# Attention stage of an image-and-text block: sums of the probabilities taken from spare columns of the values, inverses on 48x41 through memory, mask pieces in fp32r

## The reference

```python
h = concatenate([image_tokens(x), fake_quant(table)[x_txt]], axis=1)      # (32, 164, 192)
h = h + attn(layernorm(h))
h = h + kan(kan(layernorm(h), w1), w2)

def attn(x):                                  # q, k, v = x @ W + b, split in 12 heads of 16
    scores = einsum('bhqd,bhkd->bhqk', q, k) * 0.25
    scores = where(abs(i - j) <= 64, scores, -inf)
    out = einsum('bhqk,bhkd->bhqd', softmax(scores), v)
    return out.reshape(B, N, 192) @ Wo + bo
```

## Time and profile before

| | |
|---|---|
| median of 3 runs | 2768.41 us |
| profiled execution | 2763.8 us, span 2762.1 us |
| TensorE matmul busy | 2544.0 us (92% of the span) |
| VectorE busy | 1870.7 us (68%) |
| ScalarE busy | 1354.8 us (49%) |
| GpSimd busy | 242.1 us (9%) |
| mean granted TensorE clock | 0.953 |

### The profile page before, as it was taken

The page is one execution under the profiler, slowest core; times in us unless marked ns, Lnnn a source line. Parts: engine busy times, 40 slices in busy tenths (PEclk is TensorE's granted clock), DMA queues, the critical chain, the costliest instruction groups (busy, mean ns, idle before and its releaser), DMA issues.

```text
span 2762.1 us, 52306 instructions
## 1 busy us (share of the span) xinstructions
PE 2544.0 (92%) x21673; PEld 2308.9 (84%) x21673; DVE 1870.7 (68%) x2148; ACT 1354.8 (49%) x1292; POOL 242.1 (9%) x147
## 2 busy tenths in 40 slices
PE   8959985898889889559999999999999999999999
PEld 6736684776667667459999999999999999999999
DVE  7849913655556566386766767666877777777774
ACT  2238801322223223255353443537977777777771
POOL 2202201000000000031121212100000000000000
PEclk9989996988989999879999999999999999999999
DMA  3435513000000000000000000003000000000000
GB/s 113 128 90 148 139 33 136 10 17 9 17 9 17 14 12 13 14 12 24 17 27 23 17 23 17 23 28 115 28 20 23 24 20 21 25 20 20 27 16 9
DMA packets 83907, 103.44 MB, mean 37 GB/s; under 512 B 8919, under 2 KB 75111, under 8 KB 83047
## 3 DMA queue, kind: packets, MB, share of 16 engines
q1 hardware_dynamic: 80167, 90.99, 10.9%
q0 software_dynamic: 3616, 10.54, 1.5%
HBM read 71.14 MB, written 30.36 MB: 37 GB/s over the span
## 4 chain that ended last, share of the span: by engine, by line
PE 56%; DVE 1%; issue 0%; DMA 0%; POOL 0%; ACT 0%; SPq 0%; POOLq 0%; DVEq 0%
PE spline_acc L1620 31%; PE spline_acc L1603 8%; PE spline_acc L1602 8%; PE spline_acc L1604 8%; PE spline_xT L1583 0%; DMA spline_x<-h_scr 0%; DVE spline_weights_low L1327 0%; DVE spline_xn L569 0%; DVE spline_f L1360 0%; DVE spline_t L1348 0%; DVE spline_b L1343 0%; DVE spline_b L1337 0%; DVE spline_a L1332 0%; POOL spline_rstd L1299 0%; ACT spline_a L1491 0%
## 5 line engine op out<-in xcount | busy, mean ns | idle before, releaser
L1620 PE MATMUL spline_acc<-spline_weights,spline_f 128*128 128x192 f32 x5248 | 853.0, 326 | 0.0
L1620 PEld LDWEIGHTS spline_acc<-spline_weights,spline_f 128*128 128x128 f32 x5248 | 852.8, 190 | 0.0
L1368 DVE SCALAR_TENSOR_TENSOR spline_f<-spline_n,spline_b 128x2048 f32<-128x2048 f32 x164 | 376.0, 2293 | 183.7 <-PE spline_acc L1620 181.9
L1602 PE MATMUL spline_acc<-spline_f,spline_weights_high 128*128 128x328 f32 x1536 | 479.8, 312 | 7.2 <-DVE spline_f L1360 7.2
L1603 PE MATMUL spline_acc<-spline_f,spline_weights_high 128*128 128x328 f32 x1536 | 482.4, 314 | 0.0
L1604 PE MATMUL spline_acc<-spline_f,spline_weights_low 128*128 128x328 f32 x1536 | 476.2, 310 | 0.0
L1602 PEld LDWEIGHTS spline_acc<-spline_f,spline_weights_high 128*128 128x128 f32 x1536 | 289.9, 189 | 7.4 <-issue 7.4
L1603 PEld LDWEIGHTS spline_acc<-spline_f,spline_weights_high 128*128 128x128 f32 x1536 | 289.1, 188 | 0.0
L1604 PEld LDWEIGHTS spline_acc<-spline_f,spline_weights_low 128*128 128x128 f32 x1536 | 288.7, 188 | 0.0
L1360 DVE SCALAR_TENSOR_TENSOR spline_f<-spline_n,spline_a 128x984 fp32r<-128x984 f32 x128 | 151.1, 1180 | 200.1 <-PE spline_acc L1604 198.4
L912 ACT ACTIVATE attend_probs<-scores_by_key 82x1968 f32<-82x1968 f32 x64 | 115.7, 1807 | 316.2 <-PE scores_by_key L1040 316.2
(11 more groups left out here) (154 smaller groups left out, 3567.3 us busy)
## 6 DMA issues: line engine op xcount, KB each, us to landing
sample_pos<-pos_scr SPq DMA_DIRECT2D x32, 540.0 KB, 4.4
hid_scr<-spline_hid SPq DMA_DIRECT2D x64, 164.0 KB, 1.8
spline_xn<-hid_scr SPq DMA_DIRECT2D x41, 256.0 KB, 3.1
pix_scr<-stem_by_pixel SPq DMA_DIRECT2D x32, 225.0 KB, 2.5
sample_h<-pix_scr POOLq DMA_DIRECT2D x32, 225.0 KB, 4.4
spline_weights_raw<-w SPq DMA_DIRECT2D x1, 6144.0 KB, 22.0
spline_weights<-w SPq DMA_DIRECT2D x4, 1536.0 KB, 6.1
h_scr<-attend_h SPq DMA_DIRECT2D x16, 246.0 KB
```

What stands on the lines that cost most here:

```text
L1368: nc.vector.scalar_tensor_tensor(f2[i][:], n_[u][:], MAGIC + i, b_[u][:], ALU.is_equal, ALU.mult).then_inc(f_ready, 1)
L1602: nc.tensor.matmul(z, high, x_high, start=start, stop=False)
L1620: last = nc.tensor.matmul(z, f2[i][:, r * P:(r + 1) * P], w2[:, i, r, :], start=(i == 0 and r == 0), stop=(i == 3 and r == 4 * CH - 1))
```

## The change

- **Masks.** `piece` and `mask` are copied to fp32r instead of bf16, and the windows get even widths: 222 x 3 and 250 x 3 columns of the four pieces instead of 218 x 3 and 246 x 3.
- **Sums.** The 16 columns of `attend_v` that were zero beside each head's 16 values are one. The product with the values so leaves the sums in rows 16 to 31 of every group of 32; `mix(..., True)`, the tile of ones and `SUM` are gone.
- **Inverses through memory.** ScalarE copies the whole product (`mix_out`, 128x492) to `mixed[i]`. SyncE stores 4 rows of it to memory, loads them as 48x41, VectorE inverts them (one reciprocal), SyncE stores 48x41 and loads it with four transfers, each repeated over 32 rows, into `spread[i]`; VectorE then multiplies `mixed[i]` by `spread[i]` (`weigh`). Each step waits for the one before.
- **Order.** A sample is inverted and weighed in the half after its own: VectorE's `invert` after the second `maximum`, `weigh` behind `low_max`, `residual` at the end of the half. `project_out` moves from behind q = 1 to behind the second wk projection (first half) or behind `values` (second half), ahead of `mix`. The uses of the banks are renumbered, 16 for a pair.
- **Bias.** The bias of the output is a row of `wo` (row 16 of the first group, where the weighed product is sum times inverse). GpSimd's addition and `bo` are gone; the residual is loaded from memory a second time.
- **Queues.** SyncE keeps the constants, the spline weights and the round trips of the sums. GpSimd now issues, for every pair, the store of the result, three loads of the residual and three loads of the input.
- `values` moves from VectorE to ScalarE; `double` writes columns 16 to 18 instead of 3 to 5.

The core of the diff, in this order: the numbering of the banks, `invert` of SyncE, `pair` of GpSimd, of VectorE and of TensorE (behind q = 3):

```diff
-    NX = 18
+    NX = 16
+    SUMS, PART = 48, HEADS * TOK // 48
-        X, Q, K_, V = (0, 1), (3, 4, 5), (8, 9, 10), (13, 16)
-        Y, SUM, MAX, MIX = (2, 12), (6, 14), (7, 15), (11, 17)
+        X, Q, K_, V = (0, 1), (2, 3, 4), (6, 7, 9), (11, 13)
+        Y, MAX, MIX = (8, 14), (5, 12), (10, 15)
...
+            def invert(t, i):
+                sp.wait_ge(mix_ready, 2 * t + i + 1)
+                sp.dma_start(total_scr[i], mixed[i][DH:P:32, :]).then_inc(total_out[i], 16)
+                sp.wait_ge(total_out[i], 16 * t + 16)
+                sp.dma_start(total[i][0:SUMS, :], total_scr[i].rearrange("j (k n) -> (j k) n", n=PART)
+                             ).then_inc(total_in[i], 16)
+                sp.wait_ge(inverted, 2 * t + i + 1)
+                sp.dma_start(rec_scr[i].rearrange("j (k n) -> (j k) n", n=PART), rec[i][0:SUMS, :]
+                             ).then_inc(rec_out[i], 16)
+                sp.wait_ge(rec_out[i], 16 * t + 16)
+                for j in range(4):
+                    sp.dma_start(spread[i][32 * j:32 * j + 32, :],
+                                 rec_scr[i, j:j + 1, :].rearrange("a n -> (a n)").partition_broadcast(32)
+                                 ).then_inc(spread_in[i], 16)
...
+            def pair(tt, u, more=True):
+                t = 2 * tt + u
                 pool.wait_ge(ln, LN_STEPS * t + LN_VAR)
                 pool.tensor_tensor(rstd[0:ROWS, :], ve[0:ROWS, :], minus_half[0:ROWS, :], ALU.pow).then_inc(pow_done, 1)
                 if not (isinstance(tt, int) and tt == 0):
-                    pool.wait_ge(h_ready, 2 * t - 2)
-                pool.tensor_tensor(resid[u][0:ROWS], x[u][0:ROWS],
-                                   bo[0:ROWS, :, :].to_broadcast([ROWS, 4, D]), ALU.add).then_inc(resid_ready, 1)
+                    leave(t - 2, u)
+                load(pool, resid[u], resid_in[u], t)
+                if more:
+                    pool.wait_ge(xn_ready, t + 1)
+                    load(pool, x[u], x_in[u], t + 2)
...
+                    before = (t, 0) if i == 1 else None if first else (t - 1, 1)
                         if q == 1:
+                            if before:
+                                invert(*before)
+                            if i == 1 and more2:
+                                norm_out(tt + 1, u, use(t, X[1]))
...
                     if i == 0 or more:
                         low_max(use(t, MAX[i]), splits + (8 if i == 1 else 4 if more else 1))
+                    if before:
+                        weigh(*before)
+                    if i == 0 and more:
+                        for g in range(HG):
                             low_k(v, g, use(t, K_[g]), splits + 5 + g)
+                    if i == 1:
+                        residual(tt, u, 0, use(t, Y[1]))
+                    elif not first:
+                        residual(tt - 1 if u == 0 else tt, v, 1, use(t, Y[0]))
...
+                    if i == 0:
+                        if more:
+                            project(wq, 2, use(t, Q[2]))
+                        turn_max(a + 1, use(t, MAX[0]))
+                        if more:
+                            for g in range(2):
+                                project(wk, g, use(t, K_[g]))
+                        if not first:
+                            project_out(a - 1, 1, use(t, Y[0]))
+                        if more:
+                            project(wk, 2, use(t, K_[2]))
+                        read(*(start(START["V"][j]) if first else use(t - 1, V[j]) for j in range(2)))
+                    else:
+                        if more:
+                            turn_max(a + 1, use(t, MAX[1]))
+                            values(1, use(t, V[1]))
+                        project_out(a - 1, 0, use(t, Y[1]))
                     pe.wait_ge(exped, 2 * a + 2)
-                    mix(u, i, use(t, SUM[i]), True)
+                    mix(u, i, use(t, MIX[i]))
```

More of the change, by code:

```diff
@@ L710, in _ @@
+            with sp.Fori(0, PAIRS) as t:
+                for i in range(2):
+                    invert(t, i)
         @block.gpsimd
         def _(pool):
+            for u in range(2):
+                load(pool, x[u], x_in[u], u)
             pool.memset(minus_half[:, :], -0.5).then_inc(half_set, 1)
             pool.memset(mx[:], 0.0).then_inc(zeros_set, 1)
-            pool.memset(ones[:], 1.0).then_inc(ones_set, 1)
             for u in range(2):
-                pool.memset(va[u][:], 0.0).then_inc(zeros_set, 1)
+                pool.memset(va[u][:, :, :, 0:DH], 0.0).then_inc(zeros_set, 1)
+                pool.memset(va[u][:, :, :, DH:32], 1.0).then_inc(zeros_set, 1)
@@ L835, in pair @@
                         if q == 1:
[L836 to L850 removed]
+                            if before:
+                                invert(*before)
+                            if i == 1 and more2:
+                                norm_out(tt + 1, u, use(t, X[1]))
+                        if q == 2 and i == 0 and more:
+                            low_q(v, 0, use(t, Q[0]), splits + 1)
+                            low_q(v, 1, use(t, Q[1]), splits + 2)
                     if i == 0 or more:
@@ L856, in pair @@
                         low_max(use(t, MAX[i]), splits + (8 if i == 1 else 4 if more else 1))
-                    if i == 1 and more:
-                        values(v, 1, use(t, V[1]))
-                    for g in range(HG):
-                        invert(g, use(t, SUM[i]))
-                        if i == 0 and more:
+                    if before:
+                        weigh(*before)
+                    if i == 0 and more:
+                        for g in range(HG):
                             low_k(v, g, use(t, K_[g]), splits + 5 + g)
-                    weigh(2 * t + i, use(t, MIX[i]))
+                    if i == 1:
+                        residual(tt, u, 0, use(t, Y[1]))
+                    elif not first:
+                        residual(tt - 1 if u == 0 else tt, v, 1, use(t, Y[0]))
             norm_in(0, 0)
@@ L870, in _ @@
                 low_k(0, g, start(START["K"][g]), HG + g + 1)
-            for i in range(2):
-                values(0, i, start(START["V"][i]))
             for q in range(4):
@@ L885, in _ @@
             pair(PAIRS // 2 - 1, 1, more=False, more2=False)
-            residual(1, 1, use(PAIRS, Y[0]))
+            invert(PAIRS - 1, 1)
+            weigh(PAIRS - 1, 1)
+            residual(PAIRS // 2 - 1, 1, 1, use(PAIRS, Y[0]))
         @block.scalar
@@ L913, in expo, with pair @@
                                      ACT.Exp, scale=SCALE).then_inc(exped, 1)
-            def pair(tt, u, more=True):
+            def pair(tt, u, first=False, more=True):
                 t = 2 * tt + u
@@ L923, in pair @@
                     expo(2 * t + i, 1)
-                    if i == 0 and more:
-                        for g in range(2):
-                            high(qh[:, g, :], use(t, Q[g]))
-                    if i == 0 and more:
-                        high(qh[:, 2, :], use(t, Q[2]))
-                    sums(use(t, SUM[i]))
+                    if more:
+                        if i == 0:
+                            for g in range(HG):
+                                high(qh[:, g, :], use(t, Q[g]))
+                        else:
+                            values(v, 0, use(t, V[0]))
                     if i == 0 or more:
                         high(mh[:], use(t, MAX[i]))
-                    if i == 0 and more:
-                        for g in range(HG):
-                            high(k1[v][:, g, :], use(t, K_[g]))
+                    if more:
+                        if i == 0:
+                            for g in range(HG):
+                                high(k1[v][:, g, :], use(t, K_[g]))
+                        else:
+                            values(v, 1, use(t, V[1]))
+                    mix_out(2 * t + i, i, use(t, MIX[i]), first)
             for i in range(2):
@@ L941, in _ @@
                 high(k1[0][:, g, :], start(START["K"][g]))
+            act.wait_ge(zeros_set, 5)
+            for i in range(2):
+                values(0, i, start(START["V"][i]))
             high(mh[:], start(START["MAX"]))
-            for u in range(2):
-                pair(0, u)
+            pair(0, 0, first=True)
+            pair(0, 1)
             with act.Fori(1, PAIRS // 2 - 1) as tt:
```

204 lines of the change are left out of this document (87 added, 117 removed).

## The result

The kernel after takes **2902.02 us** (median of 4 runs, 2894.11 to 2909.21) against 2766.26 us for the kernel before in the same series: a ratio of **1.050** [1.046, 1.054]. It is slower, as forecast, but by 136 us between the medians where 42 were predicted (2810 against 2768), and outside the range of 2755 to 2860.

The account below looks back on a forecast made before the run. TensorE's order was taken as the frame (626 of 738 us busy in the attention stage, clock 0.89). Sum: 2763.8 + 2 (pairs) + 35 (clock) - 4 (start) + 13 (end) = 2809.8, say 2810 us; range 2755 to 2860.

Parts of the forecast that it names:

- the removed sums come back as waits: TensorE, both halves of a pair: the 1.81 us of sums in each half return as waits; 16 pairs +2 us.
- The waits of 0.9 and 1.0 ahead of q = 2 and q = 3: TensorE, second half: new waits for VectorE's second and third maximum, 0.9 and 1.0 us.
- the total without trip and masks: Whole kernel: pairs +2, clock +35, start -4 and end +13 us, with round trip and masks at 0.
- the clock's +35: TensorE, attention stage: two more slow stretches a pair at 1.1 us, granted clock below 0.85; +35 us, bounds 0 to +72.
- the start was forecast at -4: Start of the stage: inputs asked for first on GpSimd, which no longer adds the residual; -4 us.
- the +13 forecast for the last half and the bare trip: End of the stage: the last trip stands bare and the last second half lengthens; +13 us, bounds 8 to 20.
- Round trip. Hidden, with 1.3 us to spare, so 0.: Sums through memory: hops of 1.5 to 2.2 us finish before weigh; 0, a 3 us hop up to 2 a half.
- GpSimd or the trip late: Rival, chance 0.15: power late or spread after 13.2, shifting norm_out and later maxima; 2840 to 2870 us.
- GpSimd's 0: GpSimd, second half: seven DMAs issued ahead of norm_out's power, ready at 6.2 when needed by 6.4; 0 us.
- masks 0: Key masks on TensorE in fp32r: no cost, as most groups stand before a shrinking wait; bounds 0 and 13 us.
- Clock holds: Rival, chance 0.20: the new waits on TensorE come but don't lower its clock; 2775 us, no change within 0.5%.
- Faster: Rival, chance 0.14: TensorE's removed sums all come back if VectorE's second-half chain is 1.5 us shorter and bank free; 2702 us.

Follow-up runs that it names:

- e8: The kernel of e7 with each transfer of 82 or 46 rows cut in two (80 and 2, 32 and 14): 1.0237, +66 us.
- e9: The kernel of e8 with the masks back in bf16 and their windows odd again: 1.0166, +46 us.
- e2: The kernel after without GpSimd's loads of input and residual and stores of the result in the loop: 1.0272, +75 us.
- e3: The kernel after without the round trip of the sums and the inverse, weighing by a constant tile, GpSimd's transfers kept: 1.0224, +62 us.
- e1: The kernel before with only the mask pieces in fp32r and the even windows: 1.0037, +10 us.
- e10: The kernel of e9 with output projection and residual back behind q = 1, for sample a - 2 instead of a - 1: 1.0053, +15 us.
- e12: The kernel of e11 with norm_out at the end of the second half, behind the weighing, and the input's load behind the second trip: 0.9653, 2668.82 us.
- e11: The kernel of e10 with, in second halves, the projection behind q = 0 and the second part of values ahead of turn_max: 0.9897, -28 us.
- e7: The kernel after with GpSimd's transfers moved uncut to SyncE's queue, behind the spread of each pair's first sample: 1.0346, +96 us.

## Why the prediction was right and wrong

**Right: that the removed sums come back as waits.** First half: waits of 0.25, 0.6 and 1.65 us were forecast, 0.18, 0.58 and 1.53 came. Second half: 1.3 ahead of q = 1 came as 1.28, and 1.45 ahead of `turn_max` as 1.48. The waits of 0.9 and 1.0 ahead of q = 2 and q = 3 do not show where the trip is on time (e8): at 1.2 GHz TensorE arrives later itself; in e9 one of 0.56 us stands ahead of q = 2.

**Right in sum, partly by luck: the total without trip and masks.** Forecast 46 us, e9 shows 46, with an error of some 10. Whether the clock's +35 is right was not measured by itself; from 540 to 1100 us the granted clock is 0.91 before, 0.74 after and 0.78 in e9, so the sign (below 0.85) came. The forecast saw two more slow stretches a pair at 1.1 us; in e8 one of them takes most of a second half (about 872 to 886 us). That it still comes to the same total is luck in part: the start was forecast at -4, but the first maximum starts at 452.38 before and 452.40 after, with the stage before it 0.9 us sooner, so nothing was gained. At the end of the stage the way from the third last residual to the last takes 27.2 us before (1125.58 to 1152.82) and 36.8 after (1241.88 to 1278.70): +9.6 against the +13 forecast for the last half and the bare trip.

**Wrong: "Round trip. Hidden, with 1.3 us to spare, so 0."** This is the failed step: not 0, but 71 us by e8 and 62 by e2. The durations were 1.5 to 2.2 us a hop, from two loads of constants elsewhere in the program. In the second half the hops took 3.4 and 7.1 us, because the change issues 246 KB of stores and 492 KB of loads just ahead of them. The step itself named the price of a late hop ("up to 2 us a half"), and the error is to have taken it from a row without traffic. The rival "GpSimd or the trip late" (2840 to 2870) had half of the mechanism: it let the trip be late at the spread, where the load of the sums was late, and it put the rest on GpSimd's issues. These took 8.4 us instead of 7. In the kernel after the power was just in time behind the late sums; with the trip gone (e3) it is up to 2.3 us late in some pairs, 1.9 if the inverse's 0.4 is set against it, so GpSimd's 0 was wrong as well, hidden by the larger error. The rival should have been in the sum, not beside it.

**Wrong, within its bounds: masks 0.** 10 us (bounds 0 to 13). The argument that they stand before a wait that shrinks did not hold: e1's time grew by as much as the six groups a sample did (9.6 us).

**The rivals.** *Clock holds* is out: 0.74. *Faster* did not come in the change as made, but its condition was named rightly, that VectorE's chain in the second half be shorter and the bank be free: e10 to e12 make both true, with the projection and the transfers moved too, and give 2669 us. Of the clock these traces show that gaps of 1.3 to 1.6 us stand ahead of stretches at 1.2 GHz, and that in e12, without them, their share falls from 42% (e9) to 16%. The Trainium skill, "TensorE: Matmul & The Clock Gate", section "Why this matters for your kernels", warns of longer idle gaps; the prediction found none in the pair that it read, but TensorE's idle times at the loop's turns, 2 to 3 us in every kernel, are nearly of that kind, with the clock low for 10 us and more behind each in e12. They are there before and after alike, so they explain none of the loss; the shorter gaps are what the change added. Of the port, GpSimd's seven issues took 8.4 us in the kernel after and as much in e3: their number ahead of the power made it late, and no run here shows VectorE holding them up, as the rule of the Trainium skill, "SBUF — State Buffer", section "SBUF: two separate sides", would have it.

## What to carry to other kernels

Take the duration of a small transfer that something waits for from a row with the traffic that it will run beside; if the change itself adds that traffic, put it where no small transfer is under way, and look at how fast it drains, not only at its bytes: nearly the same bytes ran at 45 or at 112 GB/s by how the rows were cut (e7, e8). Work that leaves the bounding engine is only worth something once each wait that it uncovers is filled with other due work: here the same sums and inverses gave 5.0% more time in one order and 3.5% less in another, with the transfers placed elsewhere and the masks back in bf16. Count the waits of over a microsecond on TensorE, for what they cost in clock comes on top of what they cost in time (some 40 us on top of 26 from e11 to e12, by subtraction).

## What was not expected of the hardware

- Cutting 82 rows into 80 and 2 (and 46 into 32 and 14) made the issue of the load behind them on the same queue 0.33 us instead of 3.31, and was worth 30 us in the kernel, with an error of some 16 (e7, e8).
- At the start of the stage VectorE's scaling of the norm (L569, four operations) took 2.79 us in place of 1.24 while GpSimd issued three loads (433.71 to 437.0), though those write another tile. In e2 and e3, which issue them there too, it took 2.79 as well; without GpSimd's issues (e8) it took 1.24 at the same place:

```profile
434.56 2.79 DVE L569 TENSOR_SCALAR attend_xn<-attend_x,attend_mv,attend_rstd 82x192 f32<-82x192 f32 x4
```
```profile
434.36 1.10 POOL L686 DMA_DIRECT2D attend_resid<-txt_scr  x1
435.46 1.54 POOL L687 DMA_DIRECT2D attend_resid<-txt_scr  x1
```
